# Third layer's norm and the fourth layer's projections in one block of work

## The reference, cut to what matters

```python
x = _layernorm(x + _L2_gnn_ref(x, L2_gnn_W, L2_gnn_b, src, dst, edge_weight), axis=-1)   # layer 3
x = _layernorm(x + _L3_gnn_ref(x, edge_index, L3_gnn_W, ...), axis=-1)                   # layer 4

def _layernorm(x, axis=-1, eps=1e-05):
    m = jnp.mean(x, axis=axis, keepdims=True)
    v = jnp.var(x, axis=axis, keepdims=True)
    return (x - m) / jnp.sqrt(v + eps)

# the start of layer 4
xp = (x @ W).reshape(N, H, C)                    # 128 -> 8 heads of 16
a_src = jnp.einsum('nhc,hc->nh', xp, att_src)    # 8 values of a node as a source
a_dst = jnp.einsum('nhc,hc->nh', xp, att_dst)    # 8 values of a node as a target
```

## Time and profile before

| | |
|---|---|
| time, median of 3 executions | 9360.04 us (9357.07 to 9362.92) |
| profiled execution, span from first to last instruction | 12999.9 us |
| time of the profiled execution outside that span | not given; the span stands for it |
| mean granted TensorE clock | 0.787 |
| PE busy in the span | 9231.9 us (71%) |
| DVE busy in the span | 6869.4 us (53%) |
| POOL busy in the span | 5674.7 us (44%) |
| ACT busy in the span | 3183.5 us (24%) |
| the norm stage, 9794.4 to 9878.8 us of the span | 84.4 us |
| the projection stage, 9878.8 to 9980.0 us of the span | 101.2 us |

### The profile page before, as it was taken

The page is one execution under the profiler, slowest core; times in us unless marked ns, Lnnn a source line. Parts: engine busy times, 40 slices in busy tenths (PEclk is TensorE's granted clock), DMA queues, the critical chain, the costliest instruction groups (busy, mean ns, idle before and its releaser), DMA issues. The chain is left out here.

```text
span 12999.9 us, 294862 instructions
## 1 busy us (share of the span) xinstructions
PE 9231.9 (71%) x88712; PEld 7531.3 (58%) x88762; DVE 6869.4 (53%) x25269; ACT 3183.5 (24%) x9441; POOL 5674.7 (44%) x5790
## 2 busy tenths in 40 slices
PE   5977777777777777677777774888873555555555
PEld 5866667776766667634454453666662444444443
DVE  8964444444444444456666665555544555555555
ACT  5841111112111111241111123111113233222223
POOL 3534444442444444305555551444442555555552
PEclk8888888888888888789999996888886555555555
DMA  1013333333333333462222223333332111111113
GB/s 50 28 47 90 91 89 89 88 90 105 90 89 90 89 88 90 95 217 69 67 67 66 67 70 110 101 104 102 101 94 70 39 39 39 39 39 39 39 39 61
DMA packets 962709, 999.47 MB, mean 77 GB/s; under 512 B 141701, under 2 KB 861933, under 8 KB 962093
## 3 DMA queue, kind: packets, MB, share of 16 engines
q1 hardware_dynamic: 774502, 616.47, 17.1%
q0 software_dynamic: 174720, 364.70, 12.9%
q10 hardware_dynamic: 13255, 16.19, 0.4%
HBM read 858.52 MB, written 144.69 MB: 77 GB/s over the span
## 5 line engine op out<-in xcount | busy, mean ns | idle before, releaser
L497 POOL DMA_INDIRECT ring<-att_table,idx x1592 | 1556.3, 978 | 1307.7 <-ACT idx L484 715.5
L1225 PE MATMUL psum<-ring 128*128 128x128 bf16 x21276 | 1547.8, 226 | 784.6 <-issue 766.3
L1225 PEld LDWEIGHTS psum<-ring 128*128 128x128 bf16 x21276 | 1281.3, 101 | 984.9 <-issue 927.9
L1162 DVE TENSOR_SCALAR ring<-sel,iota_col 128x640 bf16<-128x640 bf16 (+1 forms) x1576 | 487.0, 369 | 2368.2 <-remote 1627.6
L1240 PE MATMUL psum<-state 64*128 64x128 f32 x14112 | 1479.8, 356 | 208.9 <-issue 206.7
L1240 PEld LDWEIGHTS psum<-state 64*128 64x128 f32 x14112 | 1318.1, 261 | 345.7 <-issue 330.0
L1148 POOL DMA_INDIRECT ring<-gcn_table,idx x980 | 932.3, 951 | 1300.6 <-ACT idx L1197 996.0
L1679 POOL DMA_INDIRECT state<-rel_table,state x1120 | 1071.1, 956 | 981.8 <-ACT state L1779 657.6
L1148 POOL DMA_INDIRECT ring<-rows,idx x980 | 933.7, 953 | 1289.0 <-ACT idx L1197 993.2
L1169 DVE TENSOR_SCALAR state<-iota_row,state 128x128 f32<-128x128 f32 x5488 | 1457.2, 356 | 0.0
L1394 POOL DMA_INDIRECT state<-hyp_table,state x784 | 755.8, 964 | 855.3 <-ACT state L1471 650.6
(11 more groups left out here) (447 smaller groups left out, 15814.7 us busy)
## 6 DMA issues: line engine op xcount, KB each, us to landing
ring<-xparts SPq DMA_DIRECT2D x1332, 192.0 KB
ring<-srow SPq DMA_DIRECT2D x544, 128.0 KB
sel<-drow SPq DMA_DIRECT2D x394, 160.0 KB
sel<-drow SPq DMA_DIRECT2D x394, 128.0 KB
rel_table<-tout SPq DMA_DIRECT2D x98, 512.0 KB, 2.6
ring<-att_table,idx POOLq DMA_INDIRECT x1592
ring<-rows SPq DMA_DIRECT2D x56, 448.0 KB
xparts<-state SPq DMA_DIRECT2D x28, 672.0 KB, 3.6
```

Source lines behind the costliest of these rows:

```text
L497: pool.indirect_dma_start(out=ring[:, u, k, 0:width], out_offset=None, in_=table, in_offset=bass.IndirectOffsetOnAxis(ap=idx[:, u, k:k + 1 ...
L1162: ins = nc.vector.tensor_scalar(reach[u % 2][:, t, :], wanted[u], at[:, :], None, ALU.is_equal)
L1225: last = nc.tensor.matmul(rowsP[v][:, j * P:(j + 1) * P], reach[v][:, t, j * P:(j + 1) * P], xwin[u][:, t, i, :], start=(t + i == 0), stop ...
```

## The change

A new block, `norm_into_attention`, does the work of both stages for each block in one loop with one fence behind it. Each engine's list is made of steps of the same block number with different leads. `lagged` writes `lead` steps ahead of the loop, a loop of 8 steps (4 turns of 2), and 6 steps behind it; `block_at` turns a step and a lead into the block worked on. A semaphore that is raised once or twice ahead stands for blocks that don't exist.

The leads, in blocks: SP loads (`load`) 5 ahead, stores the rows (`keep`) 2 ahead and the table (`keep_table`) at 0. ACT normalises (`normalised`) 2 ahead and then copies the target values (`keep_target`) at 0. PE transposes (`transpose_block`) 2 ahead and then takes products (`product`) 1 ahead. DVE takes the reciprocal (`normalise`) 2 ahead, the transposed rows (`columns`) 1 ahead, the sums (`sums_and_spread`) 3 ahead and the table rows (`table_rows`) at 0, in this order.

The normalised rows go to `stage`, not back to `acc`. Both PE's transposes and SP's store to `rows3` read them there, so that ACT now waits for both before it writes the buffer again (`rowsT` and `kept0`/`kept1`). The copy of `acc` to `stage` (L2206) is gone.

```diff
+        def lagged(eng, step, lead):
+            for b in range(-lead, 0):
+                step(0, b)
+            with eng.Fori(0, NB // 2 - 3) as it:
+                step(it, 0)
+                step(it, 1)
+            for b in range(NB - 6, NB):
+                step(b // 2, b % 2)
+        def norm_into_attention():
...
+                    def load(it, u):
+                        sp.wait_ge(sem("summed"), b + 1)
+                        sp.dma_start(tiles(xblk[:, v, :]), rows_of(rows2, b)).then_inc(sem(f"xin{v}"), 16)
+                    def keep(it, u):
+                        sp.wait_ge(sem("normed"), b + 3)
+                        sp.dma_start(rows_of(rows3, b), tiles(stage[:, v, :])).then_inc(sem(f"kept{v}"), 16)
+                    def keep_table(it, u):
+                        sp.wait_ge(sem("tB"), b + 2)
+                        sp.dma_start(rows_of(att_table, b), tiles(tout[:, v, 0:BT * ROW5], ROW5)
+                                         ).then_inc(sem(f"tstored{v}"), 16)
...
+                    def normalised(it, u):
+                            act.wait_ge(sem("var"), b + 1)
+                            nc.scalar.activation(sd[:, v, :], mv[:, v, :, 1], ACT.Sqrt, bias=eps_t[:, :]
+                                                 ).then_inc(sem("sdev"), 1)
+                            act.wait_ge(sem("scaled"), b + 1)
+                            act.wait_ge(sem("rowsT"), b + 1)
+                            act.wait_ge(sem(f"kept{v}"), turn * 16 + 16)
+                            for t in range(BT):
+                                last = nc.scalar.activation(stage[:, v, t * P:(t + 1) * P],
+                                                            acc[:, bass.ds(b * BW + t * P, P)], ACT.Identity,
+                                                            bias=shift[:, v, t:t + 1], scale=rstd[:, v, t:t + 1])
...
+                    def transpose_block(it, u):
+                            pe.wait_ge(sem("normed"), b + 3)
+                            pe.wait_ge(sem("xTfree"), b + 1)
...
+                    def product(it, u):
+                            pe.wait_ge(sem("xTready"), b + 1)
+                            pe.wait_ge(sem("tB"), b + 1)
...
+                            pe.wait_ge(sem("saved"), b + 1)
...
+                    def step(it, u):
...
+                        normalise(it, u)
+                        columns(it, u)
+                        sums_and_spread(it, u)
+                        table_rows(it, u)
...
-            residual_norm("hyp", rows2, rows3 if layers > 3 else out)
+            if layers > 3:
+                norm_into_attention()
+            else:
+                residual_norm("hyp", rows2, out)
         if layers > 3:
-            project("att")
             attention()
```

More of the change, by code:

```diff
@@ L2467, in project, with block_at, is_block @@
             fence()
+        def lagged(eng, step, lead):
[6 more added lines that the diff above has]
+                step(b // 2, b % 2)
+        def block_at(it, u, lead):
+            at = u + lead
+            return it * 2 + at, at % 2, it + at // 2
+        def is_block(b):
+            return not isinstance(b, int) or 0 <= b < NB
```

130 lines of the change are left out of this document (added).

## The result

| | before | changed | ratio, 95% interval |
|---|---|---|---|
| median of the first comparison | 9358.56 us (4 executions) | 9282.6 us (4) | 0.9919 (0.9905 to 0.9933) |
| median of the second, on one chip | 9357.65 us (15) | 9284.94 us (5) | 0.9924 (0.9911 to 0.9938) |
| the two stages in the trace | 183.4 us | 116.2 and 115.5 us | |
| the attention in the trace | 2075.4 us | 2071.1 and 2069.6 us | |

The change makes the kernel 73 to 76 us faster by the medians; the interval of the second comparison allows 58 to 83 us.

The account below looks back on a forecast made before the run. Norm bound by DVE, projections by PE, in sequence; merged, DVE sets the pace. 3.9 + 16.1 + 85.8 + 14.7 = 120.5 us against 180.9, so 60 us off 9360 gives 9300 us; range 9292 to 9324.

Parts of the forecast that it names:

- full step: Merged loop: one block through DVE's four parts, 7.28 us plus 0.5 us of gaps, 7.8 us; ends 7.3 and 8.3.
- The two old stages: Norm and projections before the change, from the norm's first load to the end of the last table rows: 180.9 us.
- is the same after the change: Row factor, the table's last store, the fence and clearing `acc`, around the two stages: claimed unchanged, so given no saving.
- the drain: End of the merged block: three steps without sums, DVE waiting for products, 4.88 us each, 14.7 us in all.
- the first load: Start of the merged block: the first load, before DVE can begin its sums, 3.9 us.
- the ramp: Merged block behind its first load: three partly filled steps of 4.3, 5.3 and 6.5 us, together 16.1 us.
- the better end: Largest saving kept for the two stages, 66 us, with loop steps of 7.3 us; 60 us was the forecast.
- From the span to the median: Whether the profiled saving holds in unprofiled runs: taken in full, 60 us, rather than shrunk to 43 us.
- The DMA: Merged loop: part of a 17% rival; mixed loads and stores at 152 GB/s bind, 9.3 us a step, 9316 us.
- The lag: Merged loop: products of a block are ready before DVE reaches its table rows, with 1.5 us of slack.
- rival 3: Merged loop: a missed meeting puts everything in sequence, 15.6 us a step, 9385 us; slower from 13.3 us; chance 4%.
- the 3.5 us: Last three steps: if PE's clock is low, each takes 6.0 rather than 4.9 us, 3.5 us lost in all.

## Why the prediction was right or wrong

**What failed.** Three terms of the sum were off, all to the same side. The full step was put at 7.8 us and measured 7.43 on average, since 0.5 us of gaps had been added that are not there: 4 us. The two old stages were put at 180.9 us and took 183.4: 2.5 us. The attention behind got no term at all, under "is the same after the change", and was 4 to 6 us shorter. The first two make nearly all of the way from the 60.4 us forecast to the 67.5 measured in the two stages. That alone would have given 9360 − 67.5 = 9292.5 us, at the very edge of the range; it is the attention, whose cause is open, that took the time clearly out of it. What is left to the 76 us of the first comparison, some 3 us, was not found again in the second.

**The bound, right.** DVE's list sets the pace of the merged loop. Taking 14.8 us of work off DVE gained 15.1; adding 16.5 us to PE cost 5.7, about 4.8 of it in the drain.

**The sum of the new block, 120.5 us forecast, 116.2 measured.** By its terms: the first load 3.9 (measured 3.9); the ramp 16.1 (15.9, to the end of the third run of sums); eleven full steps 85.8 (81.7); the drain 14.7 (14.8). The term that was mis-sized is the full step, 7.8 us forecast against 7.42 in the loop and 7.0 in the steps written out. The four parts came out near what they were priced at: sums 4.29 (4.29), reciprocal and shift 0.40 (0.37), copy with its wait and what follows 1.57 (1.34), table rows 1.16 (1.28), together 7.42 (7.28). But I added 0.5 us for gaps between them, and only 0.14 us came on top: the copy of the table rows gives way to the next reciprocal after 1.16 us, and the wait between copy and sums was 0.47 us where I had 0.25. 11 × 0.4 is 4 us.

**The 180.9 us to which it was compared: 183.4 in a profile of normal length.** One more block of the projections and the first products met the low clock. That is 2.5 us of the miss. The prediction says that the clock of the projections "fell once"; in the trace that it read, three blocks of table rows already followed the last by 7.9 to 8.0 us. Together the stages give 67.5 us, beyond the 66 that I kept as the better end: the new block's step of 7.43 us was not even at that end's 7.3, but the end had nothing for scatter in the old stages.

**What lies behind "is the same after the change", wrong by about 5 us.** What the prediction names there did stay: `acc` was cleared 6.0 us after the last table rows began, before and after. The attention, which it does not price, took 2075.4 us in the kernel before and 2078.5 in the one without table loads, but 2069.6 to 2072.3 in all six profiles of kernels with the changed block and a lead of two on DVE. With the copy on ACT or a lead of one it took 2075.9 to 2085.1. Its instructions are the same in all but one. It belongs to the kernel more than to the execution (two executions of one kernel differ by 1.5 us), and its cause is open. It would account for the 73 us in the median where the stages give 67.5, and for the 7 to 9 us of the 15 more with the copy on ACT. That is a sum that fits, not an experiment, and the time ahead of the stages scatters by more.

**From the span to the median, right.** I took the saving in full and not at 0.72, since the rows looked unstretched. The norm stage took 84.4 us in the execution of 12999.9 us and in that of 9361.4.

**The range** was too narrow below: 9292 stood 8 us under the forecast and 24 us lay above. A shorter step had been allowed for, but a slower old stage and a shorter attention had not.

**The rivals.** The DMA did not bind, at 165 GB/s and not at 191 either. The lag held, and the runs with a lead of one show what it is worth: 79 us in the two stages with DVE's order kept, which made the kernel slower than before, by the mechanism of rival 3 (though DVE there waits for the transposes and not for the products). There the step was 13.5 us, just beyond the 13.3 from which that rival was to decide.

**The clock.** It was 0.83 in the merged block, with some steps at either level: in 5 of the 14 blocks the products of the table rows took 2.7 to 3.5 us rather than 1.86. That cost 0.8 us at most in the full steps. The last three steps ran at a granted clock of 1.00, so the 3.5 us that the prediction weighed for them were not lost. In the run with a lead of one and DVE's order kept, PE idles for 7 us a step, its granted clock is 0.73, and the products take 5.4 us and not 3.5. The rule of the Trainium skill (TensorE: Matmul & The Clock Gate, "HAM oscillation — how this bites in real kernels"), that PE starts again at the slow clock behind such a pause, agrees with that run and with the slow products of the merged loop; the 3 us that the sum was to lose by it don't show.

## What to carry to other kernels

When two stages bound by different engines are merged, write down the bounding engine's list for one step, add its parts without gaps except where a register or a wait stands, and then ask of each hand-over what other work of the waiting engine lies between. Lead and order must be looked at together. With DVE's order kept, one block of lead decided between 75 us faster and 16 us slower; but with the shorter lead, one swap in DVE's order gave back 59 of the 79 us. With the longer lead the place of the sums and the table rows mattered less: in a cycle (table rows, products, table rows) the products have the same time whatever the order of the other work, and that swap cost 8.7 us. And check that a trace is of the length of the timed executions before its saving is set against them; where it isn't, compare work that should not have changed.

## What the runs showed of the hardware

- PE's clock and the step's length can feed on each other. In the run with a lead of one and DVE's order kept, PE idled 7.2 us a step and came back with products of 3.51 us rather than 1.86, for which DVE had to wait. With twice the products PE was granted 0.90 over the block, the highest of the runs with that order of DVE, and the step stayed at 7.43 us.
- The same attention code took 2069.6 to 2085.1 us with changes only in the stages ahead of it, and differed by 1.4 and 1.5 us between two executions of one kernel. PE's clock in it (0.67 to 0.79) does not explain this.
- One profiled execution of the kernel before was 39% longer than its timed ones, without a longer norm stage (84.4 us in both), and a later one was not.
